# A head loop's setup rearranged: the first head's weights split in pieces, the second head's maxima taken earlier, preparation work behind each step's maximum

## The reference

```python
x = x + _L0_attn_ref(_layernorm(x, axis=-1), L0_attn_w_qkv, L0_attn_w_o)
...
scores = jnp.einsum('bhqd,bhkd->bhqk', q, k) / jnp.sqrt(jnp.float32(D_HEAD))
probs = jax.nn.softmax(scores, axis=-1)
...
# NF4 rounding of a weight (first part)
scalers_1 = jnp.max(jnp.abs(blocks), axis=1)
scaler_mean = scalers_1.mean()
centered = scalers_1 - scaler_mean
s_absmax = jnp.max(jnp.abs(sb), axis=1, keepdims=True)
...
# ternary rounding of c_fc and c_proj
scale = jnp.maximum(jnp.mean(jnp.abs(w)), EPS)
```

## Time and profile before

| what | value |
|---|---|
| median of 3 runs | 916.41 us (916.15 to 917.59) |
| the profiled execution, its own time | 914.14 us |
| its span in the profile | 912.3 us |
| PE busy | 848.8 us (93%) |
| DVE busy | 707.6 us (78%) |
| ACT busy | 539.0 us (59%) |
| POOL busy | 373.0 us (41%) |
| mean granted PE clock | 0.994 |

### The profile page before, as it was taken

One profiled execution on the slowest core, in us unless ns is written; L12 is line 12 of the kernel. 1 busy time (PEld: TensorE's weight loads), 2 busy tenths in 40 slices (PEclk: granted clock), 3 DMA queues, 4 the chain that ended last, 5 costly groups with the idle time before them and its releaser, 6 DMA issues. The chain is left out here.

```text
span 912.3 us, 18715 instructions
## 1 busy us (share of the span) xinstructions
PE 848.8 (93%) x6868; PEld 630.7 (69%) x6868; DVE 707.6 (78%) x1749; ACT 539.0 (59%) x1285; POOL 373.0 (41%) x358
## 2 busy tenths in 40 slices
PE   6888998999999999999999998999978889999786
PEld 3555766777777777777777776887855578777554
DVE  5647967887788788877887774997688779886985
ACT  1655576665666566656665655464566864546676
POOL 6014555545555555545554644052242031522410
PEclk9999999999999999999999999999999999999999
DMA  9133131101110111011100000000000010000001
GB/s 279 40 83 93 22 94 36 31 6 35 35 26 8 35 35 35 0 35 35 35 0 11 1 1 2 2 1 1 1 1 1 1 47 1 1 1 1 1 1 47
DMA packets 34723, 25.56 MB, mean 28 GB/s; under 512 B 9492, under 2 KB 31596, under 8 KB 34668
## 3 DMA queue, kind: packets, MB, share of 16 engines
q1 hardware_dynamic: 34380, 24.56, 10.1%
q10 hardware_dynamic: 288, 0.26, 0.1%
HBM read 22.65 MB, written 2.17 MB: 27 GB/s over the span
## 5 line engine op out<-in xcount | busy, mean ns | idle before, releaser
L502 POOL CAST exp_hi<-exp_scores 128x1024 f16<-128x1024 f32 x64 | 67.0, 1047 | 199.4 <-ACT exp_scores L628 199.4
L504 POOL TENSOR_TENSOR exp_lo<-exp_scores,exp_hi 128x1024 f16<-128x1024 f32 x64 | 140.7, 2198 | 5.1
L628 ACT ACTIVATE exp_scores<-banks,exp_bias,unscale 128x256 f32<-128x256 f32 x256 | 141.0, 560 | 2.1
L75 PE MATMUL banks<-value_out_hi,xn_t_hi 128*128 128x256 f16 x512 | 139.6, 273 | 0.8 <-DVE X L961 0.5
L76 PE MATMUL banks<-value_out_lo,xn_t_hi 128*128 128x256 f16 x512 | 139.5, 273 | 0.0
L77 PE MATMUL banks<-value_out_hi,xn_t_lo 128*128 128x256 f16 x512 | 139.5, 273 | 0.0
L1119 PE MATMUL banks<-qk 128*128 128x256 f32 x512 | 121.6, 380 | 8.5 <-ACT exp_scores L628 8.4
L1119 PEld LDWEIGHTS banks<-qk 128*128 128x128 f32 x512 | 96.6, 190 | 29.4 <-issue 8.7
L961 DVE SCALAR_TENSOR_TENSOR X<-banks,colsum,X 128x256 f32<-128x256 f32 x256 | 106.2, 478 | 12.8 <-DVE colsum L952 11.4
L573 ACT ACTIVATE qk<-banks 128x512 f32<-128x512 f32 x128 | 75.8, 601 | 58.9 <-PE banks L77 58.9
L75 PE MATMUL banks<-xn_t_hi,head_weights_hi 128*128 128x512 f16 x256 | 96.9, 378 | 2.4 <-ACT qk L573 1.6
(11 more groups left out here) (254 smaller groups left out, 1962.4 us busy)
## 6 DMA issues: line engine op xcount, KB each, us to landing
head_weights<-in_wqkv_d SPq DMA_DIRECT2D x32, 128.0 KB, 3.8
weight_absmax_rows<-across_partitions SPq DMA_DIRECT2D x15, 256.0 KB, 4.2
X<-in_x_d SPq DMA_DIRECT2D x4, 512.0 KB, 7.6
head_weights<-in_wqkvt_d SPq DMA_DIRECT2D x16, 128.0 KB, 3.5
head_weights<-in_w_o_d SPq DMA_DIRECT2D x16, 128.0 KB, 3.5
out<-X SPq DMA_DIRECT2D x8, 256.0 KB, 2.1
ternary_then_kv_and_rows<-in_c_fc_d SPq DMA_DIRECT2D x1, 1024.0 KB, 5.0
ternary_then_kv_and_rows<-in_c_proj_d SPq DMA_DIRECT2D x1, 1024.0 KB, 8.0
```

The costliest lines, as they stand in the source:

```text
L75: nc.tensor.matmul(out, lhs[0], rhs[0], start=first, stop=False)
L502: nc.gpsimd.tensor_copy(probh[:, s1_.par], prob[:, s1_.par]).then_inc(exph_ready, 1)
L504: nc.gpsimd.tensor_tensor(probl[:, s1_.par], prob[:, s1_.par], probh[:, s1_.par], ALU.subtract).then_inc(expl_ready, 1)
L628: last = nc.scalar.activation(prob[:, s1_.par, t, :], sc_ps[t // ST][:, t % ST, :], ACT.Exp, bias=nbias[:, t:t + 1], scale=unscale[:, s1_. ...
```

## The change

It touches only the setup and the written-out steps, on four queues.

- **ACT, setup.** `split_hi(0, 0, a)` at tiles 5 and 9 becomes four single scalings (`first_scaled`, at t = 5, 6, 9, 10) and two copies (`first_hi`, at t = 7 and 11). The last `key_values` and head 0's `value_out_hi` move from ahead of step 0 into step 1, behind the exponentials of step 0; `key_values` stands ahead of step 1's copies of the projection, `value_out_hi` behind them.
- **DVE, setup.** Head 1's `absmax` moves from step 0 into the tile loop (t = 9). `statistics(3)` changes places with `scales(0, 0)`. The third `block_max` moves from t = 12 to t = 11.
- **DVE, steps.** All preparation work is a function `preparation(i)`, called behind the row maximum and ahead of the column sums and the update of X; it stood behind both. `block_sums` moves ahead of head 0's `value_out_lo`. Mask words go from step 6 to 7, the hidden scale from 6 to 8.
- **SP.** Head 1's maxima are spread ahead of the block maxima and gathered behind them. Head 2's loads go from ahead of the block maxima to behind their regrouping DMA. The load of c_fc goes behind the spread of the block sums.

```diff
@@ SP @@
         for dst, src in g.early_loads:
             sp.dma_start(dst, src).then_inc(early_loaded, 16)
-        load_prepared(2, 0)
...
+        sp.wait_ge(amax_ready, 2)
+        sp.dma_start(spread(1, P, 4), amax[:, 1, :]).then_inc(amax_out, 16)
         sp.wait_ge(block_max_ready, 3)
         for mine, flat in by_column(s1t, g.scratch[0]):
             sp.dma_start(flat, mine).then_inc(s1_out, 16)
+        sp.wait_ge(amax_out, 32)
+        sp.dma_start(arows[:, 1].rearrange("p q s -> p (q s)"), gathered(1, P, 4)).then_inc(amax_in, 16)
         sp.wait_ge(s1_out, 16 * 5)
         sp.dma_start(s1[:, :, :], by_super(g.scratch[0])).then_inc(s1_in, 16)
-
-        sp.wait_ge(kv_ready, NP)
-        sp.dma_start(tf[0].rearrange("p (k n) -> p k n", k=KT), view(g.dram["c_fc_d"])).then_inc(loads_t, 16)
-        absmax_to_all(1, 2)
+        load_prepared(2, 0)
+
         sp.wait_ge(nsum_ready, 2)
         sp.dma_start(spread(2, RB, 3), srow[:, :]).then_inc(nsum_out, 16)
         sp.dma_start(spread(3, P, 2), smax[:, :]).then_inc(nsum_out, 16)
+        sp.wait_ge(kv_ready, NP)
+        sp.dma_start(tf[0].rearrange("p (k n) -> p k n", k=KT), view(g.dram["c_fc_d"])).then_inc(loads_t, 16)
@@ ACT @@
-            if t in (5, 9):
+            if t == 5:
                 act.wait_ge(w_loaded[0], 64)
                 act.wait_ge(wscale_ready, 1)
-                split_hi(0, 0, t // 8)
-        key_values(NP - 1)
-        act.wait_ge(m_full, 1)
-        value_out_hi(0)
+            if t in (5, 6, 9, 10):
+                first_scaled((5, 6, 9, 10).index(t))
+            if t in (7, 11):
+                first_hi(t // 8)
...
             if known(i) and i == 1:
+                key_values(NP - 1)
                 score_rows(1, 1)
+                act.wait_ge(m_full, 1)
+                value_out_hi(0)
@@ DVE, setup @@
-        scales(0, 0)
+        statistics(3)
...
             if t == 3:
-                statistics(3)
-            if t in (8, 10, 12):
+                scales(0, 0)
+            if t in (8, 10, 11):
                 dve.wait_ge(loads_n, 80)
-                block_max(t // 2 - 4)
+                block_max((8, 10, 11).index(t))
+            if t == 9:
+                dve.wait_ge(w_loaded[1], 64)
+                absmax(1)
@@ DVE, steps: behind the row maximum, ahead of the column sums @@
             if known(i) and i == 1:
+                block_sums()
                 dve.wait_ge(mhi_ready, 1)
                 value_out_lo(0)
...
-            if known(i) and i == 0:
-                dve.wait_ge(w_loaded[1], 64)
-                absmax(1)
+            if known(i):
+                preparation(i)
             if r is not None:
                 level_part(r, c - FIRST)
```

More of the change, by code:

```diff
@@ L316, in later_head @@
         return c % NP == k and (not known(i) or i // NP >= 1) and runs(i, 0)
-    SUM_ABS, TERNARY, ROUNDING = (3, 4), 6, (7, 8)
+    SUM_ABS, TERNARY, MASKS, HIDDEN, ROUNDING = (3, 4), 6, 7, 8, (7, 8)
     LIN_MAX, KV_MAX, LIN_SCALE, KV_HI = 1, 5, 9, FIRST + ROUNDS * BODY
@@ L573, in score_rows, with first_scaled, first_hi @@
                 nc.scalar.activation(qk[:, par, s, :], qk_ps[s], ACT.Copy).then_inc(qk_ready, 1)
+        def first_scaled(s):
+            scaled = nc.scalar.activation(wst[:, 0, s, :], wst[:, 0, s, :], ACT.Copy, scale=wsc[:, 0, s:s + 1])
+            if s % 2:
+                scaled.then_inc(wscaled, 1)
+        def first_hi(a):
+            act.wait_ge(wscaled, a + 1)
+            nc.scalar.activation(whi[:, 0, 2 * a:2 * a + 2], wst[:, 0, 2 * a:2 * a + 2], ACT.Copy).then_inc(whi_ready, 1)
         for t in range(NT - 2):
@@ L969, in step, with preparation @@
+        def preparation(i):
             if i == 2:
                 scale_codes()
-            if i == FIRST - 1:
-                dve.wait_ge(rep_in, 16 * 5)
-                dve.wait_ge(divide_ready, 1)
             for n in range(2):
@@ L1011, in step @@
                 nc.vector.tensor_scalar(g.tscale255[:, :], g.tscale[:, 1:2], 1.0 / 255.0, None, ALU.mult)
+            if i == MASKS:
                 dve.wait_ge(mask_loaded, 16)
@@ L1018, in step @@
                 nc.vector.tensor_scalar(g.maskb[:, :, :], g.maskf[:, :, :], -NEG, NEG, ALU.mult, ALU.add)
+            if i == HIDDEN:
                 dve.wait_ge(smax_ready, 1)
```

109 lines of the change are left out of this document (54 added, 55 removed).

## The result

| | before | changed |
|---|---|---|
| median, same chip | 917.0 us (916.15 to 918.3, 4 executions) | 909.13 us (908.97 to 909.59, 4 executions) |
| the profiled execution | 914.14 us | 909.0 us |
| its span | 912.3 us | 907.2 us |
| mean granted PE clock | 0.994 | 0.990 |

The ratio is 0.9915, with a 95% interval of 0.990 to 0.9931: the changed kernel is faster, by 7.9 us of median. The forecast was 906.2 with a range of 901.5 to 911.0; the time lies in the range, 2.9 us above the forecast. The two profiled executions are only 5.1 us apart, because the one of before stands 2.9 under its median and the one of the changed kernel 0.1. Lines of the changed kernel have other numbers (scores L1134 for L1119, update of X L1038 for L961).

A forecast was written before the change was run, and what follows sets the result against it. PE is full in the head loop, so gains lie in PE's idle time and clock in setup and steps: 3.6 + 12.5 - 3.9 - 0.3 - 1.7 = 10.2 us off, giving 906.2 us, range 901.5 to 911.0.

The forecast's parts named there:

- (d): Step 2: sums come late, A over 70.5; gain 1.2 if as late as before, half way 911; chance 0.12.
- Setup: Before head 0's first projection: 1.1 shorter wait, 1.7 clock drop gone, 1.0 second split, 0.2 net loss: 3.6 us off.
- (f): Setup: ACT pieces buy nothing, as something beside the split holds PE's 37.16 transpose; 1.1 to 2.8 less; no chance given.
- (c): Setup: the clock drop stays, as the gap of 1.3 is still there; 1.7 less, 907.9; chance 0.1.
- Waits of 12.5 us that can go: Scores 0 to 11: 12.5 us of waiting, nearly all before scores that wait for ACT's exponentials; all can go.
- The new wait in step 2: Step 2: PE's value matmuls wait for X's update behind the scale codes; 3.9 us, ends 2.1 and 7.3.
- A: Step 2: time the gathered rows of sums arrive, 67.1 us taken between 65.3 and 70.5; new wait is A - 63.2.
- Clock drop behind it: After step 2's new wait: one drop of PE's clock, costing 1.7 us, from below 0.
- Step 9: Step 9: linear scales and a clamp ahead of X's update cost 0.3 us, from below 0, from above 2.24.
- (a): Step 2: the new wait comes but the clock stays; 11.9 us off, 904.5; chance 0.2.
- (b): Step 2: no new wait; 15.8 us off, 900.6; chance 0.1.
- (e): Step 2: slower, A beyond 79.2, wait over 16.0; 914.5 us plus what is beyond; chance 0.02.

The follow-up runs named there:

- Run 1: Changed kernel with head 0's weight split back in two lumps of ACT work after tiles 5 and 9: 913.75 us.
- Run 11: Changed kernel refitted: scale codes in step 3, maxima, sums, masks and scales moved to other steps, linear scales in step 8 ahead of the clamp: 899.73 us.
- run 3: Changed kernel with scale codes in step 4 instead of 2, and maxima, second sum, ternary scales and masks moved to suit: 904.71 us.
- runs 9: Changed kernel with head 2's four loads (512 KB) issued on SP behind the gather of sums and maxima: 909.25 us.
- run 10: Changed kernel with head 2's loads and also c_fc's 1 MB issued behind the gather of sums and maxima: 909.21 us.
- run 8: Changed kernel with head 1's maximum back in step 0 and its spread issued behind the block maxima's DMAs: 911.49 us.
- Run 6: Changed kernel with 26 unused matmuls of 128x512 added on PE in front of its wait for X in step 3 of PE's count: 908.02 us.
- run 7: Changed kernel with the linear scales ahead of the clamp within step 9: 907.37 us.
- run 2: Changed kernel with preparation work back behind the update of X, setup and SP's queue as changed: 908.36 us.

## Why the prediction was nearly right

The direction, the setup's mechanism and the place of the new wait came out; the sum was 10.2 us off the profiled execution, and 5.1 came. That is half, and it lies outside the forecast's own ends of 6.8 and 13.6. The number is in its range partly by luck: the medians differ by 7.9. The prediction's own sign for (d), scores 2 to 3 over 15 apart, came too (15.54). Term by term:

- **Setup, 3.6 predicted, 4.07 measured.** Gap of 1.3: 1.12. Clock drop gone: yes. The second split's 1.0: the wait is gone. The net loss of 0.2 at the end: 0.80 is left, no loss. Run 1 shows that the three belong together and hang on ACT's pieces; counted from the same transpose they are worth 3.95. Rival (f) falls. Rival (c), a clock drop that stays, fell too: 39 to 43 us is at 1.00 in every profile of a run with the pieces. The lower clock at 28 to 36 us in five of these twelve is a different one, and what sets it off stayed open.
- **Waits of 12.5 us that can go.** Nearly all of them were said to stand before scores that wait for exponentials; those were 7.5 of the 12.5, and 1.61 for the copy of the projection and 1.60 for POOL's inverses stood beside them. They went, apart from 0.44 at scores 2 (0.28 of it a wait) and 0.13 at scores 1. Run 11 shows that 11.0 of the 12.5 can really be had.
- **The new wait in step 2, 3.9 predicted, 5.86 measured: the first step that failed.** Its place, its cause (run 3) and its form, A plus a fixed tail, were right; A was 69.4 instead of 67.1. Spread and gather took together what they were given (9.97, 9.9 predicted). The start was 0.5 earlier than predicted, the block maxima to the regrouping took 0.84 more, and the regrouping 1.88 more (4.88 for 3.00), the mis-sized piece above all. I had taken it from an old row in which nothing large was under way. Now head 1's gather of 256 KB stood ahead of it; the profile puts 9.9 us from its issue at 48.61 to its landing, so it was under way until 58.5, and the sum came at 59.04. That this is the cause fits, and runs 9 and 10 exclude head 2's loads. In run 8 the gather left only 0.37 ahead of the regrouping and took 4.8 to its landing, at 60.3; the sum came at 60.69, again just behind it. No run takes the gather away, so the cause is argued and not shown. The spread, on the other hand, took 3.79 behind 512 KB and 4.05 without: the far end of 7.3, where the prediction's reading of the Trainium skill's rule (DMA: Bandwidth & Descriptors, queues, rings and completion order) put it, was not seen. Those 512 KB had nearly landed when the spread went out at 59.44 (the last of the four, issued at 56.02, took 4.5 us).
- **What the formula lacked.** POOL's split from 68.38 to 70.51 holds DVE's mean: with rows 1.0 earlier, in run 10, X was ready at the same time behind POOL's split and the wait was the same. So between rows at 68.4 and at 69.4 the wait is flat. At A = 67.1 part of the chain would have run ahead of the split; what would have been left of the 3.9 no run shows. The prediction read DVE's chain as DVE's alone, though its own 3.66 for the codes had such a hold in it (the mean's 0.40 at 76.98 in the kernel before).
- **Clock drop behind it, 1.7 predicted, 2.3 measured** (15.54 - 7.34 - 5.86). Run 6 puts it at 2.1 by filling the wait. The Trainium skill (TensorE: Matmul & The Clock Gate, HAM oscillation) was right that such a drop is due behind a gap of this kind.
- **Step 9, 0.3 predicted, 2.74 measured (10.08 - 7.34): the second step that failed.** I had added durations of DVE and left room for them. The amount of work was right: in run 7, which only changes the order, 0.28 is left (7.62 - 7.34). The other 2.46 are the two holds, 1.94 for the one scale that stood behind POOL's split (2.10 instead of 0.16) and 0.52 for line 921 behind its cast. In the kernel before, this work stood behind the update of X and held up the next row maximum instead; the 3.21 that I took for it has 0.57 of such a hold in it (0.74 instead of 0.17).

The misses on the steps are 2.0 + 0.6 + 2.4 + 0.6 = 5.6; the setup's 0.5 goes against it, which makes the 5.1 between 10.2 and 5.1. That the medians differ by 7.9 and not by 5.1 comes from the kernel before: its profiled execution was 2.9 faster than its median. The mean granted clocks of its executions bear on this. Of the 37 that were timed beside the runs, the eleven at 0.993 or 0.994 took 914.0 to 917.1 us, the six at 0.986 took 921.1 to 922.2, and the middle one 917.04 at 0.991; the profiled one had 0.994. A clock lower by 0.003 over 912 us is 2.7 us, an estimate, which is nearly the 2.9. So its usual execution seems to lose the time to clock drops that the profiled one didn't have; where they stand no trace shows.

Of the rivals, (d) was nearest in its mechanism: A at 69.4 is just inside the range given for the forecast (65.3 to 70.5). Its condition, A over 70.5, was not met. (a), (b) and (e) fell: the clock did drop, the wait was there, and A was far from the 79.2 that (e) asks for.

## What to carry to other kernels

Small work on the engine that feeds the others goes where the data it needs are already there: moving it ahead of the critical operation put 8.3 us of waits for X in the place of the 5.9 us of waits for exponentials and POOL that run 2 has, and only placing each piece by its own due time (run 11) paid. Long activations that stand ahead of a copy on a critical chain can be worth cutting into pieces: that alone brought 3.95 us here, by shorter waits of PE and by the clock drop that no longer followed one. When a chain's time is added up from rows, look at what POOL runs beside it: a DVE instruction of one element per partition can last as long as POOL's. Rows of an old trace can hold such a stretch already, so each row of a chain is compared with the same instruction elsewhere before it is added.
